# First attention's loop in another order: score waves later, value products before the fourth and sixth pairs, roundings in three batches

## What is computed

```python
x = x + tanh(g_xattn[0]) * L0_xattn(layernorm(x), ctx)   # 16 heads of 16: the part changed here
x = x + tanh(g_ffn[0])   * L0_ffn(layernorm(x))          # one of 8 experts for each token
x = x + tanh(g_xattn[1]) * L1_xattn(layernorm(x), ctx)   # ternary weights, rounded activations
x = x + tanh(g_ffn[1])   * L1_ffn(layernorm(x))          # 16 experts mixed, then attention
```

```python
scores = einsum('bnhd,bmhd->bhnm', q, k) / 4
attn = softmax(scores, axis=-1)                  # over the 361 context vectors
out = einsum('bhnm,bmhd->bnhd', attn, v)         # then W1, relu, W2
```

## Time and profile before

| | |
|---|---|
| median of three executions | 615.0 us |
| the profiled execution | 616.17 us |
| its span, first to last instruction | 614.4 us |
| TensorE busy | 597.2 us (97%) |
| VectorE busy | 326.6 us (53%) |
| ScalarE busy | 218.2 us (36%) |
| the loop, iterations 0 to 7 | 59.6 to 183.3 us |

### The profile page before, as it was taken

One profiled execution on the slowest core, in us unless ns is written; L12 is line 12 of the kernel. 1 busy time (PEld: TensorE's weight loads), 2 busy tenths in 40 slices (PEclk: granted clock), 3 DMA queues, 4 the chain that ended last, 5 costly groups with the idle time before them and its releaser, 6 DMA issues.

```text
span 614.4 us, 9623 instructions
## 1 busy us (share of the span) xinstructions
PE 597.2 (97%) x3759; PEld 408.7 (67%) x3759; DVE 326.6 (53%) x787; ACT 218.2 (36%) x511; POOL 76.2 (12%) x75
## 2 busy tenths in 40 slices
PE   9999999999999999999999899999999999999997
PEld 7665444454456777999999568777565555555587
DVE  2986767488775745222222779885462233231554
ACT  3554655646673364222112376662200010001000
POOL 0062100003005202322221000001001000000000
PEclk9999999999999969999999899998999999999999
DMA  8920000102001663999995000700722832320000
GB/s 189 311 86 18 1 1 1 36 2 55 2 1 27 205 200 108 328 336 352 328 346 222 20 2 4 237 2 5 261 83 99 317 103 77 103 77 1 0 28 27
DMA packets 25579, 70.63 MB, mean 115 GB/s; under 512 B 5254, under 2 KB 13030, under 8 KB 21702
## 3 DMA queue, kind: packets, MB, share of 16 engines
q1 hardware_dynamic: 21910, 58.16, 28.9%
q0 software_dynamic: 3632, 11.97, 5.8%
HBM read 64.62 MB, written 5.49 MB: 114 GB/s over the span
## 4 chain that ended last, share of the span: by engine, by line
PE 83%; DVE 6%; ACT 5%; DMA 3%; issue 1%; POOL 1%; SPq 1%; DVEq 0%
PE bank L2106 21%; PE bank L1601 10%; PE bank L1754 7%; PE bank L1939 7%; PE bank L1926 7%; PE bank L2142 7%; PE bank L1728 5%; PE bank L1772 3%; DMA region<-in_ctxT 2%; PE bank L1697 2%; ACT region L1493 2%; PE bank L1760 2%; PE bank L2060 2%; DMA stage<-x_slots,token_of 1%; PE bank L1582 1%
## 5 line engine op out<-in xcount | busy, mean ns | idle before, releaser
L2106 PE MATMUL bank<-region,kvT 128*128 128x400 f32 x384 | 130.4, 500 | 0.0
L2106 PEld LDWEIGHTS bank<-region,kvT 128*128 128x128 f32 x384 | 72.4, 190 | 54.2 <-issue 0.3
L1167 DVE TENSOR_TENSOR region<-xT,stage 128x800 f32<-128x800 f32 x30 | 29.7, 991 | 70.1 <-PE bank L2106 70.0
L731 DVE TENSOR_REDUCE nmax<-bank 100x2 f32<-100x722 f32 x64 | 55.2, 904 | 15.4 <-PE bank L1728 14.9
L1926 PEld LDWEIGHTS bank<-stage,region 128*128 128x128 f32 x448 | 52.1, 192 | 1.4 <-issue 0.8
L1926 PE MATMUL bank<-stage,region 128*128 128x128 f32 x448 | 52.4, 275 | 0.5 <-ACT stage L1428 0.5
L1939 PE MATMUL bank<-region,stage 128*128 128x256 f32 x224 | 50.7, 379 | 0.0
L1939 PEld LDWEIGHTS bank<-region,stage 128*128 128x128 f32 x224 | 41.5, 190 | 5.1
L2142 PE MATMUL bank<-region,kvt 128*128 128x200 f32 (+1 forms) x192 | 44.5, 389 | 0.3 <-DVE region L1193 0.3
L1754 PE MATMUL bank<-xT,kvt 64*121 64x400 f32 (+1 forms) x144 | 39.2, 547 | 1.5 <-ACT kvT L1407 0.6
L2142 PEld LDWEIGHTS bank<-region,kvt 128*128 128x128 f32 x192 | 33.5, 190 | 9.3 <-DVE region L1193 0.6
(11 more groups left out here) (352 smaller groups left out, 940.1 us busy)
## 6 DMA issues: line engine op xcount, KB each, us to landing
region<-in_e_w SPq DMA_DIRECT2D x28, 1024.0 KB, 5.5
kvT<-in_p_qkv SPq DMA_DIRECT2D x32, 384.0 KB, 3.1
stage<-w_dram POOLq DMA_DIRECT2D x2, 1600.0 KB, 12.6
stage<-in_t_f SPq DMA_DIRECT2D x1, 2048.0 KB, 15.6
kvt<-in_p_o SPq DMA_DIRECT2D x1, 2048.0 KB, 8.9
stage<-in_e_b SPq DMA_DIRECT2D x14, 128.0 KB, 7.4
region<-in_ctxT SPq DMA_DIRECT2D x3, 541.5 KB, 14.8
stage<-w_dram POOLq DMA_DIRECT2D x1, 1200.0 KB, 8.1
```

The lines of the kernel that those rows point to most:

```text
L731: dve.tensor_reduce(nmax[:, b % 2, at_h:at_h + 9:8], banks[0:N, bank:bank + 2, 0:M], AX.X, ALU.max, negate=True)\
L1167: dve.tensor_tensor(x_w[n % NW], xT[:, :, at_h], w_bc[h][:, None, e, :].to_broadcast([P, 2, HT]), ALU.mult).then_inc(S["xw_done"], 1)
L2106: ins = pe.matmul(psum[3 * h + j][:, 0:HT], p_w[n % NP][:, k, j * HE:(j + 1) * HE], x_w[n % NW][:, k, :], start=e == 0 and k == 0, stop=e ...
```

## The change

On TensorE, within one iteration: the second, third and fourth score waves go from in front of pairs 2, 3 and 4 to in front of pairs 3, 4 and 5. The two calls of `values` that stood in front of the third pair go in front of the fourth (ahead of the third wave), and the two in front of the fifth go in front of the sixth. On VectorE the eight roundings of a batch, which stood behind each of the four waves of iterations 4 and 5, become four in iteration 4 (three behind waves 0 to 2, the fourth behind `split_maxima`), two in iteration 5 and two in iteration 6, behind waves 0 and 1. No instruction is added or removed.

```diff
+            def requantise(b):
+
+                quantise(qc[:, :, b], ctx_a[:, :, b], ctx_a[:, :, b], 4).then_inc(S["requantised"], 1)
+                if b == B - 1:
+                    dve.wait_ge(S["requantised"], B)
+                    dve.sem_inc(S["quantised"], 1)
+
             for n in range(B + 1):
...
-                    if n in (4, 5):
-                        b = 4 * (n - 4) + w
-                        quantise(qc[:, :, b], ctx_a[:, :, b], ctx_a[:, :, b], 4).then_inc(S["requantised"], 1)
-                        if b == B - 1:
-                            dve.wait_ge(S["requantised"], B)
-                            dve.sem_inc(S["quantised"], 1)
+                    if n == 4 and w < 3:
+                        requantise(w)
+                    if n in (5, 6) and w < 2:
+                        requantise(2 * n - 6 + w)
                     if n == B - 1:
                         ternarise_f1(w)
                 if n + 1 < B:
                     split_maxima(n + 1)
+                if n == 4:
+                    requantise(3)
                 if n >= 1:
                     normalise(n - 1)
...
                 for u in range(12):
-                    if u == 2:
-                        if n >= 2:
-                            turn_heads(n - 2)
-                        if n + 1 < B:
-                            score_wave(n + 1, 1)
-                    if u in (4, 6) and n + 1 < B:
-                        score_wave(n + 1, u // 2)
+                    if u == 2 and n >= 2:
+                        turn_heads(n - 2)
+                    if u == 4 and n + 1 < B:
+                        score_wave(n + 1, 1)
                     if u == 4 and n == B:
                         first_product(0, 1)
-                    if u in (4, 8) and 1 <= n <= B:
+                    if u in (6, 10) and 1 <= n <= B:
+                        values(n - 1, u // 2 - 3)
                         values(n - 1, u // 2 - 2)
-                        values(n - 1, u // 2 - 1)
+                    if u in (6, 8) and n + 1 < B:
+                        score_wave(n + 1, u // 2 - 1)
                     if n < B and u % 2 == 0:
                         score_pair(n, u)
```

## The result

| | kernel before | changed kernel |
|---|---|---|
| first comparison: median | 615.59 us (6 executions) | 610.59 us (6 executions, 609.64 to 613.14) |
| ratio, 95% interval | | 0.9926 (0.9904 to 0.9947) |
| the changed kernel a second time (e9) | 615.91 us (17 executions) | 612.35 us (12 executions), 0.9947 (0.9922 to 0.9972) |
| all executions of the study: median | 615.35 us (93) | 611.76 us (18) |
| profiled execution | 616.17 us | 610.34 us |

What follows compares the result with a forecast made beforehand. TensorE, busy 97%, was taken as the bound, with gains only from its short waits. Profiled 616.17 less 2.36 of waits and 1.5 of clock gave 612.3, the median 615.0 - 2.4 gave 612.6; forecast 612.4 us, range 610.4 to 614.9.

Steps and rivals of the forecast that it cites:

- Rules A and B: TensorE's earliest starts: a wave's follower 0.84 us after the preceding maxima end (A); a pair's, 1.08 after the needed exponential (B).
- the hand timeline: Loop iterations laid out by steps and rules, first pair to turned values: 14.40, 13.67, 13.63, 12.45, 14.40, 14.40 us for 1 to 6.
- The sum of the waits: TensorE's waits removed less new ones, iterations 2 to 6: 0.17 + 0.81 + 0.62 + 0.36 + 0.40 = 2.36 us.
- of which 0.25 is lost to a slower clock: Iteration 4 before: 0.25 of its 13.32 us put down to the slower clock, leaving 0.62 gained.
- The clock: Behind iteration 3 in the profiled execution: clock expected full instead of 0.50, worth 1.5 us.
- The new waits of iteration 3: Rival: clock falls anyway at iteration 3's fourth wave (0.84 lost) or second pair; 613.8 us, chance 0.15.
- The first rival: The median before also loses the slow stretch behind iteration 3: 615.0 - 2.4 - 1.5 = 611.1 us, chance 0.20.
- The median as mostly free of the slow stretch: Median before, 615.0, taken as mostly without the slow clock, since the profiled execution stood 1.2 above: 612.6 us.
- The roundings: VectorE's roundings moved across iterations 4 to 6: none late; a late one would cost up to 1.3 us.
- Mode changes: TensorE's array mode changes around values and pairs: +-0.1 us, seven times, so +-0.7; taken as 0.
- The waits only move: Rival: third wave's maxima later, fourth wave waits 0.84 in seven iterations, 2.1 more: 614.8 us, chance 0.14.
- slower: Rival: fourth wave's later maxima and split delay the next turned maxima beyond 1.6 us slack: 618.5 us, chance 0.06.

Runs made afterwards that it cites:

- e9: The changed kernel, measured again unchanged beside the kernel before: median 612.35 us, ratio 0.9947 to before, loop 118.03 us.
- e5: The kernel before, measured again unchanged: median 614.80 us, ratio 0.9998 to before, loop 121.23 us.
- e8: Changed kernel with waves and values reordered on TensorE so that something other than a chain unit stands between all pairs: 610.15 us, ratio 0.9918 to before.
- e4: Changed kernel with the values back in front of the third and fifth pairs, so only waves and roundings moved: 614.87 us, ratio 0.9990 to before.
- e7: Changed kernel with the old order in iteration 3 alone: 612.04 us, ratio 0.9951 to before.
- e2: Changed kernel with the old order on TensorE, so only the roundings moved: 617.19 us, ratio 1.0025 to before.
- e1: Kernel before with TensorE's new order and the old roundings: 612.79 us, ratio 0.9955 to before, loop 119.18 us.
- e3: Kernel before with only the values moved, to in front of the fourth and sixth pairs: 616.40 us, ratio 1.0009 to before.
- e6: Kernel before with TensorE's new order in iteration 3 only: 614.25 us, ratio 0.9986 to before.
- e11: As e8, with the split ahead of the last two chain maxima on VectorE: 610.86 us, ratio 0.9916 to before.
- e10: As e11, with the rounding behind the split in iteration 4 moved in front of it: 608.38 us, ratio 0.9886 to before.

## Why the prediction was right, and where not

The time was right by its range (610.4 to 614.9 against 610.59 in the first comparison, 611.76 over all). The forecast itself, 612.4, was 1.8 above the first comparison and 0.6 above the median of all executions. The chances were less good: 0.60 lay on a difference too small to measure, and it was measured, on the faster side.

**Rules A and B, the hand timeline.** Right. Iterations 1, 2, 3, 4, 5 and 6 came within 0.03 of it, the new waits included, and iteration 7 with its 0 lost and gained came as 12.41 for 12.46.

**The sum of the waits.** Predicted 2.36, measured 121.23 - 118.03 = 3.20 between two loops at the full clock. Iterations 2, 3, 5 and 6 gave 0.19, 0.81, 0.37 and 0.42 for 0.17, 0.81, 0.36 and 0.40, and iteration 7 gave 0.05. The term that was mis-sized is iteration 4, with 0.62 predicted and 1.37 measured (13.80 - 12.43). What it was to become was right; what it was before was not. I took 13.32 less 0.25 for the clock, from a profile in which the lower clock had moved TensorE's wave behind VectorE's three scale instructions. At the full clock those stand in front of the first maxima and put a second wait of 0.70 into the iteration (e5). The step that failed is "of which 0.25 is lost to a slower clock": I subtracted the direct loss and didn't ask what the loss had hidden. Rule A, laid over the old order too, with the scales in VectorE's queue, would have shown it. Most of what iteration 4 of e8 missed is the same wait.

**The clock.** Predicted 1.5 in the profiled execution, measured 122.01 - 121.23 = 0.78: the 1.26 of the way to the next first pair, less 0.48 by which iteration 4 was shorter for it. The two errors are one, seen from both sides, and in the profiled execution they nearly cancel: 2.36 + 1.5 = 3.9 predicted, 3.98 measured in the loop. That agreement is luck. In the medians they don't: there I counted on 2.4 to 2.6 and got 3.6, near the 3.20 of the waits at the full clock; what the clock adds in them is below what they resolve.

That the clock would stay full behind iteration 3 was right in every profile. Over all of them the lower level came there in three of five with the old end of iteration 3 (before, e4, e7; not e2, e5), and in none of eight with something in front of its sixth pair (changed, e9, e1, e3, e6, e8, e11, e10). That is an association in thirteen profiles, and what decides in the five isn't known; the kernel before alone had it in one of its two profiles. The new waits of iteration 3, which I feared for the clock, were never followed by the lower level. In time the lower level doesn't show: e6, which changes only that iteration, has a median 0.9 to 1.1 below before's, with 0.8 from its wait alone. The first rival, that the median too loses the 1.5, is thus not borne out, although its 611.1 is near the result; a share of the 0.78 in the median isn't excluded either, since e6's interval reaches from 2.0 us faster to 0.2 slower.

**The median as mostly free of the slow stretch.** Left open. Executions of the kernel before ran from 613.4 to 619.9, and those with a lower mean clock over the whole span were longer (0.981: 617.1 on average in 21; 0.986: 614.3 in 18), but a mean over the span doesn't say where the stretches lay. In the thirteen profiles most of the time at the lower clock, 10 to 20 us, is behind the loop.

**The roundings.** "None is late" was right for the new order, and e1 shows that they matter: 1.15 of the loop would be lost without them. I had counted them at nothing in the sum. They are at nothing only against the kernel before, where the old order leaves the old roundings room (1.65 and 1.61 at the two places where e1 has 2.20 and 2.19); they are a condition of the new order.

**Mode changes.** The bound of +-0.7 wasn't needed: the stretches fit to 0.03 with the term at 0.

**The waits only move, slower.** Neither came, and no turned maxima of the loop waited for VectorE. But the point from which lateness would cost something was wrong. I gave the split 1.6 us of slack, up to the turned maxima. In iteration 5 that was about right (it ended at 149.68, they started at 151.61). Iteration 2 is shorter: there the split ended at 105.01, they started at 106.24, and GpSimd's instruction started at 105.05. The last instruction of the split was 0.27 ahead of it. By what e1 shows for that instruction, a split 0.3 us later would have been held up for a further 1.2 us, which is all the slack there was; that is an estimate, no run has the changed kernel with it. Closer still was the rounding behind iteration 4: it started 0.09 ahead of GpSimd's instruction, and in e8, 0.40 behind it, it was held up for 1.2. I didn't see either because GpSimd, at 12% busy, was in no step of my timeline.

## What to carry to other kernels

Where two engines hand banks to each other, two lines are enough for a timeline: from what a wait ends (an end, not a start) and how long after. Such a timeline was right to 0.03 us in a 14 us iteration, so lay the old order out by it as well, and ask wherever it disagrees with the profile: the row may be one of a disturbed stretch, where a slower engine hides another's wait. When steps move, lay the engines beside them out too, with the idle ones: an instruction of 0.2 us took 1.4 for meeting one of GpSimd.

## What the runs showed of the hardware

- VectorE beside GpSimd: a cast of 100x16 took 1.41 instead of 0.20 (e8, and the same in e4), a tensor-tensor of 100x16 1.46 instead of 0.23 (e1), a rounding into bf16 of 128x722 1.73 instead of 0.54 (e8, e4, e11), each while one tensor-tensor of 128x800 ran on GpSimd for 1.5 to 1.8. Maxima of 100x722 stayed at 0.9 each.
- Who started first decided who was held up: with the rounding 0.09 ahead, it took its 0.54 and GpSimd's instruction 1.83 instead of 1.52 (changed kernel, e9, e7).
- The lower granted clock (0.50) behind iteration 3 lasted 3.4 us in one profile and 6.9 and 6.8 in two others. Its price wasn't the time at half speed: 0.78 net in the profile of before, where a wait of TensorE for VectorE (0.70, e5) vanished beside it, and 2.80 in e7 for the 6.9 us.
